# Six slots with one late-layer step each in every chunk of a delta rule, in place of three slots with two

## The reference, cut to what matters

```python
x = x + 0.5 * L0_ffn(layernorm(x))          # silu(gate) * up, then down
x = x + L0_attn(layernorm(x))               # conv, silu, gated delta rule, rms norm, Wo
x = x + 0.5 * L0_ffn(layernorm(x))
x = x + 0.5 * L1_ffn(layernorm(x))          # token shift, sigmoid(r) * (relu(k)^2 @ Wv)
x = x + L1_attn(layernorm(x))               # rope, softmax in blocks of 64 tokens
x = x + 0.5 * L1_ffn(layernorm(x))
```

```python
kS = einsum('bhd,bhdv->bhv', k_t, S)
S  = a_t * (S - b_t * k_t (x) kS) + k_t (x) v_t
o_t = einsum('bhdv,bhd->bhv', S, q_t)
```

## Time and profile before

| | us |
|---|---|
| median of 3 runs | 8609.14 |
| profiled execution | 8607.54 |
| its span, first to last instruction | 8605.7 |
| mean granted TensorE clock in it | 0.894 of full |
| PE busy / weight loads busy | 6932.5 / 4998.7 |
| DVE / ACT / POOL busy | 4672.9 / 2623.3 / 2271.0 |

### The profile page before, as it was taken

How to read it: one execution, slowest core, us unless ns; L and a number is a source line. 1 busy time by engine, 2 the same in 40 slices (tenths; PEclk the granted TensorE clock), 3 DMA queues, 4 the chain that set the end, 5 groups by cost and what they waited for, 6 DMA issues and landing times. The chain is left out here.

```text
span 8605.7 us, 157131 instructions
## 1 busy us (share of the span) xinstructions
PE 6932.5 (81%) x57416; PEld 4998.7 (58%) x57416; DVE 4672.9 (54%) x10083; ACT 2623.3 (30%) x5274; POOL 2271.0 (26%) x3553
## 2 busy tenths in 40 slices
PE   7788887877878788887888878788787888878886
PEld 4665646556565565656656466565655656556564
DVE  6446464554645546565464645546455464554643
ACT  3223242332423214232242422324232142322421
POOL 1403223041321413314132230423304133141321
PEclk9888988898988888988889888889888999888997
DMA  1100101001000100001000010010000100010000
GB/s 50 33 23 20 39 14 31 26 20 44 19 20 25 28 36 19 21 29 25 33 19 25 28 31 26 19 44 19 20 26 24 39 19 20 29 25 35 19 22 3
DMA packets 376003, 225.76 MB, mean 26 GB/s; under 512 B 336880, under 2 KB 353392, under 8 KB 366960
## 3 DMA queue, kind: packets, MB, share of 16 engines
q1 hardware_dynamic: 375152, 214.71, 8.4%
HBM read 155.95 MB, written 58.72 MB: 25 GB/s over the span
## 5 line engine op out<-in xcount | busy, mean ns | idle before, releaser
L773 DVE SCALAR_TENSOR_TENSOR PS<-SC,CW,PS 128x512 f32<-128x512 f32 x1536 | 1156.3, 754 | 167.6 <-DVEq L771 75.7
L1478 PE MATMUL PS<-CST,SC 128*128 128x128 f32 x2776 | 480.6, 314 | 560.1 <-PEq L1531 258.6
L1475 PE MATMUL PS<-S,KQ 64*64 64x128 f32 x8192 | 769.2, 309 | 0.0
L1478 PEld LDWEIGHTS PS<-CST,SC 128*128 128x128 f32 x2776 | 353.8, 159 | 698.6 <-issue 680.4
L986 POOL TENSOR_TENSOR RSTD<-VAR,NHALF 128x2 f32<-128x2 f32 x200 | 143.0, 715 | 2322.9 <-POOLq L985 2177.6
L1145 POOL TENSOR_TENSOR FR<-MS,NHALF 128x8 f32<-128x8 f32 x128 | 210.1, 1641 | 1501.3 <-POOLq L1144 1298.4
L1475 PEld LDWEIGHTS PS<-S,KQ 64*64 64x64 f32 x8192 | 562.3, 156 | 73.1 <-issue 72.4
L1475 PE MATMUL PS<-XT,WV 128*128 128x512 f32 x1024 | 548.7, 665 | 58.5 <-PEq L1776 58.5
L1475 PE MATMUL PS<-XT,WQK 128*128 128x512 f32 x1024 | 559.9, 685 | 0.0
L1475 PE MATMUL PS<-SC 128*64 128x32 f32 (+1 forms) x2720 | 333.0, 334 | 264.5 <-PEq L1600 151.5
L1069 POOL TENSOR_TENSOR WO<-WO 128x30 f32<-128x30 f32 (+14 forms) x960 | 507.3, 528 | 136.4
(11 more groups left out here) (156 smaller groups left out, 12756.0 us busy)
## 6 DMA issues: line engine op xcount, KB each, us to landing
WV<-in_wv SPq DMA_DIRECT2D x16, 2048.0 KB, 11.7
WO<-in_wo SPq DMA_DIRECT2D x16, 2048.0 KB, 7.8
WQK<-in_wq SPq DMA_DIRECT2D x16, 1024.0 KB, 5.2
WQK<-in_wk SPq DMA_DIRECT2D x16, 1024.0 KB, 7.3
cells_in<-SC SPq DMA_DIRECT2D x128, 128.0 KB, 2.7
WO<-cells_in SPq DMA_DIRECT2D x32, 512.0 KB, 3.3
cells_out<-WO SPq DMA_DIRECT2D x32, 512.0 KB, 2.6
cells_nat<-WO SPq DMA_DIRECT2D x32, 512.0 KB, 3.6
```

Source lines behind the costliest of these rows:

```text
L773: op = v.scalar_tensor_tensor(y, pre[:, j:j + G], CW[:, i * TAPS + j:i * TAPS + j + 1], y, ALU.mult, ALU.add)
L1475: return nc.tensor.matmul(out_, l, r, start=start, stop=stop)
L1478: return nc.tensor.matmul(out_, in_, ident, is_transpose=True, start=True, stop=True)
```

## The change

The table becomes six slots of one step each in chunks 0 to 4, and (1, 0, 1, 0, 1, 0) in chunks 5 to 7. Each chunk holds as many steps as before. The row for what stood behind the last chunk held zeros and goes.

On PE the six slots lie: behind `old_state`; behind `output_t(c-2,0)` and `output(c-1,0)`, ahead of `solve`; behind `solve`; behind `output_t(c-2,1)` and `output(c-1,1)`; behind `new_state`, ahead of `keys_t`; and behind `keys_t`. On DVE the first four are one call ahead of `s_update`, the fifth stands between `s_update` and `keys`, and the sixth between `mean_square` and `normalise`. ACT has them beside its copies in the same order. POOL inverts two columns after each of the first five slots, in place of five after each of two.

```diff
-FILL = [(2, 2, 2)] * 5 + [(1, 1, 1)] * 3 + [(0, 0, 0)]
+FILL = [(1, 1, 1, 1, 1, 1)] * 5 + [(1, 0, 1, 0, 1, 0)] * 3
...
                     right_side(c, 1)
-                    fill(FILL[c][0])
-                    fill(FILL[c][1])
+                    fill(sum(FILL[c][0:4]))
                     if c >= 5:
                         projected(c - 5, XS[p])
                     s_update(c, 0)
                     s_update(c, 1)
+                    fill(FILL[c][4])
                     if c + 1 < CHUNKS:
                         keys(c + 1)
                     if c >= 1:
                         mean_square(c - 1)
-                    fill(FILL[c][2])
+                    fill(FILL[c][5])
...
+                for c in range(CHUNKS):
+                    for k in range(5):
+                        fill(FILL[c][k])
+                        if c < 3:
+                            substitute(1 + 10 * c + 2 * k, 3 + 10 * c + 2 * k)
                     if c == 2:
                         finish_cells()
                     if c >= 1:
+                        rms()
+                    fill(FILL[c][5])
+                rms()
...
                     fill(FILL[c][0])
                     if c >= 2:
                         output(c - 2, 0)
+                    fill(FILL[c][1])
...
                         a.activation(US[c % 2][:, 512 * x:512 * x + 512], bank(x), ACT.Copy).then_inc(u_ready, 1)
+                    fill(FILL[c][2])
                     if c >= 1:
                         square_out(c - 1, 0)
...
                         output(c - 1, 0)
+                    fill(FILL[c][1])
...
                     solve(c, 1)
+                    fill(FILL[c][2])
...
                         output(c - 1, 1)
-                    fill(FILL[c][1])
+                    fill(FILL[c][3])
...
                     new_state(c, 1)
+                    fill(FILL[c][4])
...
                         keys_t(c + 1)
-                    fill(FILL[c][2])
+                    fill(FILL[c][5])
```

More of the change, by code:

```diff
@@ L938, in recurrence @@
                         normalise(c - 1, 1)
-                fill(FILL[CHUNKS][0])
                 mean_square(CHUNKS - 1)
-                fill(FILL[CHUNKS][1])
                 normalise(CHUNKS - 1, 0)
                 normalise(CHUNKS - 1, 1)
-                fill(FILL[CHUNKS][2])
                 projected(NT - 1, XS[p])
@@ L1061, in substitute @@
             def substitute(first, last):
-                for j in range(first, last):
+                for j in range(first, min(last, SUB - 1)):
                     w = SUB - 1 - j
@@ L1115, in prepare, with rms @@
                         substitute(5 * (c - HALF) + 1, 5 * (c - HALF) + 6)
+            def rms():
+                pool.wait_ge(ms_ready, 1)
+                pool.sem_inc(ms_ready, -1)
+                q.tensor_tensor(out=FR[:, :], in0=MS[:, :], in1=NHALF[:, :], op=ALU.pow).then_inc(fr_ready, 1)
             def recurrence():
@@ L1131, in recurrence @@
                 pool.sem_inc(m_loaded, -16)
[L1132 to L1136, removed]
-                        fill(FILL[c][1])
-                    if c < 3:
-                        substitute(6 + 10 * c, 11 + 10 * c)
+                for c in range(CHUNKS):
[3 more added lines that the diff above has]
+                            substitute(1 + 10 * c + 2 * k, 3 + 10 * c + 2 * k)
                     if c == 2:
```

## The result

The changed kernel takes 8676.61 us (median of 4 runs, 8665.21 to 8677.06) beside 8609.06 for the one before. The ratio is 1.0075, 95% interval 1.0063 to 1.0088: slower by 68 us. 8708 was forecast.

A forecast was written before the change was run, and what follows sets the result against it. PE, busy 81%, was taken as the bound, with time won or lost where it waits. Front half -4.0 and back half +10.2 give +6.2 us a group, 16 times +99: 8708 us; 8 in 10 range 8595 to 8785.

The forecast's parts named there:

- Front half, -4.0: Chunks 0 to 4 and into chunk 5: the moved steps change the time by -4.0 us a group in sum.
- Chunk 1: At shift(1,0): output(0,0) fills 1.9 of its 6.28 us wait, 0.7 lost again through chunk 2; -1.2 us a group.
- Step 32: In chunk 3: DVE normalises ahead of keys and mean_square, so 1.1 of the 1.72 us wait go; -1.1 us.
- chunks 4 and 5: Moved kt no longer covers ACT's copy, +1.3 us; the 5.04 us wait becomes two as POOL's power lies open, +0.2.
- The inversion slices, 0: POOL's columns throughout: Rstd, power and inverse come sooner but PE waits for none; 0 us, bounds -1 and +0.5.
- Chunk 5, 0: In chunk 5 of the back half: the moved steps have what they need; 0 us.
- `shift(0,1)`, +2.55 and +1.7 for the clock: In chunk 6: moved ahead of its covering outputs, +2.55 us; its 3.3 us wait brings the slow clock, +1.7.
- Chunk 6 into 7, +1.6 for `keys_t` and with it +3.8: values(0,1) ahead of keys_t(7) delays normalise by 1.6 us; with shift(1,1) ahead of its outputs, projected(2) starts 3.8 later.
- Power open in chunk 7, +2.2: On DVE, values(1,1) goes ahead of mean_square(6) and no longer lies beside POOL's power; +2.2 us.
- Faster: Rival: three front-half waits end below about 2 us each, keeping PE's clock up; about 8518 us, chance 0.15.
- No change: Rival: front gives 6, back costs 6, as a 3.3 us wait brings no slow clock; about 8609 us, chance 0.11.
- Slower by more: Rival: front half gives nothing, ACT's copies and POOL's power delaying each softmax step; about 8772 us, chance 0.20.

The follow-up runs named there:

- front, fives: The front-only kernel with POOL inverting five columns after the second and fourth slots, in place of two after each of five: 8588.38 us.
- front-only kernel: The changed kernel with the steps of chunks 5 to 7 put back where they stood before the change: 8513.64 us, ratio 0.9887.
- Values only: Against the slices only kernel, just the last moved step of chunks 5 to 7 moved, values(0,1) and values(1,1) going ahead: 8745.96 us.
- PE order: The changed kernel with PE's fifth slot of chunks 5 to 7 put back behind keys_t; other engines as in the change: 8699.94 us.
- shift-only kernel: Against the slices only kernel, just the middle step of chunks 5 to 7 moved, putting shift(0,1) and shift(1,1) ahead of the outputs: 8728.74 us.
- back only: The changed kernel with the steps of chunks 0 to 4 put back where they stood before, the inversion in slices of two: 8826.60 us.
- DVE-order kernel: The changed kernel with DVE's fifth slot put back behind mean_square in chunks 5 to 7: 8638.43 us.
- slices only: The kernel before with all late steps in their old places and only the inversion's columns cut into slices of two: 8625.51 us.

## Why the prediction was right, point by point

Sign and mechanism were right; the forecast was 8708 and the result 8677, inside both ranges. The sum was +6.2 us a group and came out at +4.3. Of the signs named, all came but one: the first product of `shift(0,1)` was to take 3.6 us and takes 1.97. That the back half's sum fits so well, +10.2 for 9.9, is in part luck, since terms that were off cancel.

- **Front half, -4.0: measured -5.6.** The parts were off more than the sum. Chunk 1 was put at -1.2 and is -3.7 at its solve, of which 1.1 is gone again at the solve of chunk 2. The step that failed is the constant clock: "the rest is still long enough for the slow clock" came true in 8 groups and not in the other 8, which is worth 1.2 us in the mean. The outputs moved into the wait give 1.8, as put, and the shift starts 0.65 us sooner, which was put at nothing. (6.28 less 1.9 is 4.4 and not 4.2; it is 3.7 in the mean.) From there to the solve of chunk 3 another 3.4 us come (put at 3.2). Step 32 was right (1.41 of 1.72 gone). Step 32 and chunks 4 and 5, put at -1.1 + 1.3 + 0.2 = +0.4 together, show +0.4.
- **The inversion slices, 0: wrong.** "PE waits for neither; nobody waits for it" was read off a trace in which a wait of 5.80 us hid the inverse's return. With that wait gone the return is next in line, as front, fives shows. PE also waits for Rstd: with the slices alone changed, its wait at step 15 in chunk 0 falls from 4.77 to 4.47 us. Slices of two are worth 75 us in the front-only kernel, of which some 27 at the return, and without them the six slots would give 1.2 us a group and not 5.9. The bound of -1 was too narrow. Beside two-step slots the same slices cost 1 us: the two parts of the change only pay together.
- **Chunk 5, 0: measured some +0.5.** `oa`, step 42, stands ahead of `keys_t(6)` now, so `keys` and `normalise` come later, and `output_t(4,0)` waits 1.41 us where it waited 0.94. Values only, with this move and not the shift, has the same 0.5 of waiting from P0 to P1, and in PE order, which takes the move back, it is gone.
- **`shift(0,1)`, +2.55 and +1.7 for the clock: measured +2.9, the 0.5 of chunk 5 in it.** The wait came out at 3.22 us as worked out (3.3), and the cover lost is shown by the shift-only kernel, 2.5 us of waiting. The 1.7 didn't come here in any of the 16 groups. It does come in three of the kernels tried: in place of 3.5 us the shift takes 5.2 in shift only and in 15 groups of back only, and 6.5 in PE order.
- **Chunk 6 into 7, +1.6 for `keys_t` and with it +3.8: measured +4.7, partly by another road.** The tokens of `shift(1,1)` come 1.9 us later against P1 (put at 1.6), and the outputs stand behind the shift. But the wait of 2.2 us at that shift, on which the +3.8 rests, isn't there. From `output_t(5,0)` to `solve(7)` the change needs 3685.25 - 3680.76 = 4.5 us at the slow clock, twice the 3649.39 - 3647.03 = 2.4 of before, and `solve(7)` 2.7 in place of 1.9, so PE comes to the shift 0.9 us after its tokens. The slow clock fills the wait and costs, by these rows, only some 0.6 us beyond it (an estimate: a shift that waits starts 0.3 us behind its tokens). In shift only and in PE order, with this piece at full clock, the wait is there, 2.4 us.
- **Power open in chunk 7, +2.2: measured +2.3**, and 1.7 of it taken back by the DVE-order kernel.
- **Rivals.** Faster: it needed the three long waits to end below about 2 us each, and 3.7, 2.9 and 2.4 us are left of them. The clock stays up at `shift(1,0)` in 8 groups, but over the whole front half PE is busy 2.1 us a group longer than before. No change: its first reason came true, the wait of 3.3 us doesn't bring the slow clock, and the front half gave nearly its 6, but the back half cost 9.9 and not 6. "Slower by more" needed a front half that gives nothing; it gave 5.6. What ACT's order costs by itself no run separates. The rule on interleaving regimes of the Trainium skill, "Perfetto Trace Analysis", section "Optimization Strategy", agrees with the front half, where the front-only kernel gains 95 us, and not with chunks 5 to 7.

## What to carry to other kernels

Where one in-order engine serves a serial chain and fill, judge each moved step by what is queued between the place where it is issued and the moment its input exists: moved behind such work it gains, moved ahead of it it loses, and the same edit can do both in two chunks. A cost of zero read off a trace holds only as long as the wait that hides it; ask what is next when that wait goes. Split a tuned change by region before giving it up: this one lost 0.75% as a whole, and its front half alone won 1.13%.

## What the runs showed of the hardware

The length of a wait doesn't decide by itself the clock behind it. The plainest case lies inside one kernel, slices only: `shift(0,0)` waits 2.92 us in all 16 groups, and its two products take 3.5 us in three groups and 5.2 in the others. Two groups in a row:

```profile
2393.77 3.36 PE L1471 MATMUL PS<-SC,WKR 128*128 128x256 f32 x8 [2.92 <-PEq L1521]
...
2918.37 1.96 PE L1471 MATMUL PS<-SC,WKR 128*128 128x256 f32 x8 [2.92 <-PEq L1521]
```

Between kernels it is the same at `shift(0,1)`: after a wait of 3.21 to 3.22 us its first product took 1.97 us in the change, 2.39 in shift only, 2.88 in back only and 3.75 in PE order. Back only has the change's order of work from chunk 5 on and differs ahead of it. What in the earlier work decides isn't shown. So a term of 1.7 us for the slow clock is a chance and not a price, and the cost can also fall where PE would have waited anyway, as ahead of `shift(1,1)`.

Runs of one kernel spread as well: the four of the change over 12 us, those of front, fives over 26, and all those of the kernel before that go with these experiments over 9 (8606.61 to 8615.16).
